# Attention and mixture-of-experts block on one core: the routing starts sixteen units later, the slot lists are built over 52 units, and the last batch's output loads follow them

## What is computed

```python
xn = _layernorm(x)
# attention, 16 heads of 32: causal, with an ALiBi bias
scores = einsum('bhqd,bhkd->bhqk', q, k) / sqrt(D) - slope * |i - j|
attn = softmax(scores) @ v  ->  @ Wo.T + bo
# experts: 8, of which each token takes 2
probs = softmax(xn @ gate_w.T); topw, sel = top_k(probs, 2); topw /= sum(topw)
gate_up = xn @ w1[e].T; act = silu(g) * u; expert_out = act @ w2[e].T
ffn = sum over the two experts of topw * expert_out
out = x + attn + ffn
```

## The kernel before, in words

| step | unit |
|---|---|
| routing parts 0 to 11 | 369 to 387 |
| `rank` and part 12; parts 13, 14, 15, 16 | 393; 395, 397, 399, 401 |
| `places` and `slots` of chunks 0 to 7 | 403, 411, 417, 423, 427, 431, 435, 439 |
| `lists` of chunks 0 to 7 | 409, 415, 421, 425, 429, 433, 437, 441 |
| `listr` | 443 |
| six `oload` and `xbo` of the last batch | 474 |
| windows 0 and 1 | 482 and 496 |

## Time and profile before

### The profile page before, as it was taken

How to read it: one execution, slowest core, us unless ns; L and a number is a source line. 1 busy time by engine, 2 the same in 40 slices (tenths; PEclk the granted TensorE clock), 3 DMA queues, 4 the chain that set the end, 5 groups by cost and what they waited for, 6 DMA issues and landing times.

```text
span 1607.2 us, 35535 instructions
## 1 busy us (share of the span) xinstructions
PE 1469.5 (91%) x12763; PEld 892.2 (56%) x12763; DVE 1042.5 (65%) x2500; ACT 888.6 (55%) x2020; POOL 568.5 (35%) x595
## 2 busy tenths in 40 slices
PE   4899989998898999999899898999789999999995
PEld 2565545654565555556555466555356656656662
DVE  7887786666878767777788877777243333333331
ACT  5677686665768767676776465777122222222221
POOL 5111232121123213113222233221217777777675
PEclk9999999998999999999999899999899999999998
DMA  7355231442433255443214233145777889788893
GB/s 258 103 140 133 86 107 50 121 123 79 131 93 110 66 146 149 124 131 92 80 59 123 84 97 91 39 146 140 274 189 123 134 126 146 131 138 132 127 143 46
DMA packets 171350, 193.28 MB, mean 120 GB/s; under 512 B 87536, under 2 KB 121072, under 8 KB 171056
## 3 DMA queue, kind: packets, MB, share of 16 engines
q1 hardware_dynamic: 143760, 151.67, 34.6%
q0 software_dynamic: 26128, 37.24, 14.2%
q10 hardware_dynamic: 1296, 2.11, 0.3%
HBM read 93.45 MB, written 53.74 MB: 92 GB/s over the span
## 4 chain that ended last, share of the span: by engine, by line
PE 66%; DVE 11%; issue 6%; DMA 5%; SPq 4%; ACT 3%; POOL 2%; POOLq 0%; DVEq 0%; ACTq 0%
PE S L1224 15%; PE T L1147 11%; PE O L1163 7%; PE S L1104 5%; PE S L1136 5%; PE M L1104 4%; PE M L1255 4%; PE O L1255 4%; DVE arena L1528 4%; SPq L979 4%; PE M L1186 2%; DMA out<-arena 2%; PE S L1121 2%; DVE arena L1544 2%; PE S L1186 1%
## 5 line engine op out<-in xcount | busy, mean ns | idle before, releaser
L1528 DVE CUSTOM_DVE_ANT_0 arena<-S,cF,nsl 128x1024 f32<-128x1024 f32 (+7 forms) x512 | 413.1, 811 | 70.3 <-PE S L1136 48.5
L1725 ACT ACTIVATE arena<-arena,mneg 128x1024 f32<-128x1024 f32 (+7 forms) x512 | 395.6, 773 | 57.2 <-DVE mneg L1528 56.6
L1147 PE MATMUL T<-cF,arena 128*128 128x128 f32 x2304 | 366.3, 280 | 66.1 <-ACT arena L1742 37.3
L1742 ACT ACTIVATE arena<-T 128x512 f32<-128x512 f32 (+3 forms) x532 | 241.6, 467 | 250.7 <-PE T L1147 247.9
L1147 PEld LDWEIGHTS T<-cF,arena 128*128 128x128 f32 x2304 | 267.7, 142 | 169.3 <-issue 49.0
L1224 PE MATMUL S<-arena 128*128 x1704 | 269.8, 315 | 10.0 <-issue 9.9
L1881 POOL DMA_INDIRECT out<-arena x142 | 222.1, 1564 | 107.6 <-ACT arena L1788 57.9
L1224 PEld LDWEIGHTS S<-arena 128*128 128x128 f16 x1704 | 167.7, 98 | 109.1 <-issue 11.3
L1544 DVE COPY arena<-T 128x512 f32<-128x512 f32 (+3 forms) x300 | 153.2, 514 | 108.3 <-PE T L1147 106.5
L1163 PE MATMUL O<-arena 128*32 128x128 f32 (+1 forms) x3328 | 213.6, 333 | 6.8 <-DVE arena L1564 5.7
L1136 PE MATMUL S<-arena 96*128 96x512 f16 (+3 forms) x768 | 212.8, 331 | 3.1 <-DVE mneg L1528 1.8
(11 more groups left out here) (190 smaller groups left out, 1821.6 us busy)
## 6 DMA issues: line engine op xcount, KB each, us to landing
arena<-arena SPq DMA_DIRECT2D x192, 128.0 KB, 2.4
arena<-in_w1T SPq DMA_DIRECT2D x64, 352.0 KB, 3.5
arena<-in_x SPq DMA_DIRECT2D x64, 256.0 KB, 3.5
w_d<-arena SPq DMA_DIRECT2D x32, 352.0 KB, 2.9
arena<-w_d SPq DMA_DIRECT2D x16, 704.0 KB, 6.7
arena<-in_w2T SPq DMA_DIRECT2D x32, 256.0 KB, 2.9
out<-arena SPq DMA_DIRECT2D x32, 256.0 KB, 3.0
xn_d<-arena SPq DMA_DIRECT2D x24, 256.0 KB, 2.2
```

Of the source, the lines that this page charges most:

```text
L1147: tp = pe.transpose(z[:, (c - c0) * P:(c - c0 + 1) * P], ring[u % 4][:, c * P:(c + 1) * P], idf)
L1528: dve.tensor_tensor_reduce(ring[r][:, 0:w], SBK[o.bank["score", u]][:, 0:w], rel[:, S - w:S], nsl[:, hh:hh + 1], 3.0e38, ALU.add, ALU.min, ...
L1725: act.activation(ring[r][:, 0:w], ring[r][:, 0:w], ACT.Exp, bias=mneg[:, m:m + 1], scale=-1.0, accum_out=rs[:, k, c:c + 1]).then_inc(sems[ ...
L1742: act.activation(PT[k][:, h, to_:to_ + gap * (c1 - c0 - 1) + 1:gap, :], TB[o.bank["tr", u, i]][:, 0:n].rearrange("p (c n) -> p c n", n=P), ...
```

## The change

`routing()` is cut in two at the point where the lists begin. The first half (parts 0 to 16) begins at u = 385 instead of 369, with the same stride of two. The second half becomes a generator of its own, `lists()`, which begins at u = 428 with a stride of three. `o_steps` of the last batch begins at unit 495 instead of 474 (384 + 96 + 15 instead of 384 + 96 - 6). No instruction is added or taken away.

```diff
@@ -418,6 +418,8 @@
         yield
         add("route", 16)
         yield
+
+    def lists():
         for c in range(NT // 4):
             add("places", c)
             add("slots", c)
@@ -608,14 +610,15 @@
-        jobs.append((u0 + 96 + (9 if b + 1 < B else -6), 1, 1, u0 + 128 + 44, o_steps(b)))
+        jobs.append((u0 + 96 + (9 if b + 1 < B else 15), 1, 1, u0 + 128 + 44, o_steps(b)))
...
     split_jobs = [w_max(), w_scales(), w_split()]
-    jobs.append((32 * 11 + 17, 2, 1, 32 * 15, routing()))
+    jobs.append((32 * 12 + 1, 2, 1, 32 * 13 + 12, routing()))
+    jobs.append((32 * 13 + 12, 3, 1, 32 * 15 + 14, lists()))
     jobs.append((32 * 15 + 2, 1, 1, 32 * 15 + 4, win(0)))
```

## The result

| | before | after |
|---|---|---|
| median (11 runs each) | 1607.26 us (1600.77 to 1614.79) | 1612.44 us (1607.31 to 1619.51) |
| ratio | | 1.0034, 95% interval 1.0019 to 1.0050 |
| span of the profiled execution | 1607.2 us | 1610.7 us |

The change makes the kernel slower by 0.34%, 3 to 8 us. The profiled executions differ by 3.5 us only: that of the kernel before lies 1.7 us above its median, and single executions of one kernel lie up to 14 us apart. Of the 3.5 us, units 368 to 479 hold 2.5 and what follows unit 480 0.9.

The account below looks back on a forecast made before the run. TensorE and VectorE share the bound in the attention, VectorE through the routing. Terms -2.0 + 1.2 - 3.9 - 5.9 + 15.3 + 0.9 sum to +5.6 us, 1612.8 us against the median 1607.26; range 1603 to 1619.

Parts of the forecast that it names:

- Points 1 to 3: Units 368 to 383 lose the routing, -2.0 us; 384 to 411 get it, with 1.5 us wait for `rank`, +1.2.
- Points 4 and 5: Units 412 to 427 without lists, -3.9 us; units 428 to 443 with only chunks 0 and 1, -5.9 us.
- ruler: Last batch's units beside the same units one batch earlier, without routing or lists; priced lists at 2.1 us a chunk.
- Point 6: Units 444 to 479 get chunks 2 to 7: 2.1 us each for 2 to 4, +6.3; 3.0 each after, +9.0.
- D: Slower by clock: TensorE partly at 1.2 GHz again at `rank` or late lists, 2 us; outside the sum.
- Point 7: `listr` in unit 482, where VectorE is nearly full, costs +0.9 us.
- Point 8: Six late output loads and GpSimd's additions cost nothing; additions end near 1102, 4 us before the next `aT`.
- C: Slower by the tail: late output loads make `aT` of unit 487 wait behind `xbo`; +5 us on top, 1618 us, chance 0.07.
- the contention that the Trainium skill states: VectorE instructions with two SBUF inputs exclude GpSimd's SBUF reads; tables-to-`lists` wait over 4 us, 4.5 a chunk, sum +10.
- rival A: Faster: three units between tables and products remove 8.4 us of TensorE waits; late chunks cost 1.5 us; 1602 us, chance 0.23.
- Rival B: No change: the bounding engines' work is the same wherever it stands; 1607 us, give or take 3, chance 0.25.
- The other signs: Units 464 to 479 not under 28 us, 384 to 411 within 76 to 82; `rank` wait 1.5; late-chunk TensorE idle 1 to 2.

Follow-up runs that it names:

- lists late alone: The changed kernel with the routing back at unit 369, lists and output loads staying late: 1609.84 us, ratio 1.0015.
- tables only: The changed kernel with chunks 5 to 7 reduced to VectorE's two tables, no products or sums; executed once, units 464 to 479 take 26.7 us.
- gap of four: The kernel before with each list chunk's products at least four units behind its tables, tables at units 403 to 443: 1609.55 us, ratio 1.0017.
- routing late alone: The kernel before with the routing from unit 385 and the lists right behind at their old spacing, output loads unmoved: 1615.78 us, ratio 1.0062.
- gap late: As the kernel with four units between tables and products, but three units and lists beginning 13 units later, tables at 416 to 446: 1614.39 us, ratio 1.0040.
- rank apart: The changed kernel with `rank` and routing part 12 six units behind part 11, parts 13 to 16 six later; executed once, units 368 to 479 262.0 us.

## Why the prediction was right or wrong

It forecast 1612.8 us, and 1612.44 was measured, slower as forecast. The agreement to 0.4 us is luck: the profiled span grew by 3.5 us, not 5.6, and terms of the sum were off in both directions. At unit 480 the forecast stood at +4.7 us and the trace at +2.6. The measured 5.2 come of these 2.6, of 0.9 behind that unit, and of the 1.7 us by which the profiled execution of the kernel before lay above its median while that of the changed kernel is its median. By its own dates:

| unit begins | predicted | measured |
|---|---|---|
| 384 | 851.4 | 851.5 |
| 412 | 930.9 | 930.9 |
| 428 | 966.6 | 962.3 |
| 444 | 1003.9 | 997.3 |
| 464 | 1051.8 | 1047.6 |
| 480 | 1082.9 | 1080.8 |

- **Points 1 to 3, the routing (+1.2 - 2.0 us): right in size.** 34.8 and 79.4 us were measured for 34.7 and 79.5. The routing costs the same early and late (146.0 and 145.7 us with nothing else). The meeting at rank, sized 1.5 us with bounds 0 and 3, is worth 2.0 by the run that takes it apart. That the routing's new place was no worse than the old although it had this meeting was not in the argument; units 412 to 427 took less for it.
- **Points 4 and 5, units 412 to 443: too slow by 6.6 us.** This is the step that failed. I took the same units one batch earlier as the bare time, 35.7 and 33.1 us. The bare ones are 31.5 to 34.3 and, by 32.9 - 2.0, 30.9. So the price of a list chunk in the kernel before came out too low as well: 2.1 us by the ruler, 2.6 by the runs that leave chunks out (2.4 at the full clock). Of the 6.6 us, 3.6 are the ruler's (68.8 against 34.3 + 30.9), and 2.9 are that units 412 to 427 begin with TensorE ahead behind the late routing (31.4 against 34.3). The ruler's premise, the same weight splitting in both batches, does not hold: one batch earlier the split tiles are 704 wide, not 512, and ScalarE waits longer for their stores (9.1 us against 3.1). Its copies of turned scores stand behind that in its queue, and TensorE waits for them 6.0 us instead of 1.6. These 4.4 us are of the size of the ruler's 3.6; no run takes them away by themselves. First the ruler, 641.2 to 710.0 us, then units 412 to 443 in the run with the lists late alone, which hold two chunks:

```profile
L1605 DVE SCALAR_TENSOR_TENSOR arena<-arena,sc x8: 945/949/952, 647.1 to 705.8; 128x704 f16<-128x704 f32 x8
...
ACT arena L1761 <- DMA w_d<-arena: 9.1, 3, 4.3
...
PE T L1147 <- ACT arena L1742: 6.0, 7, 2.5
```

```profile
L1608 DVE SCALAR_TENSOR_TENSOR arena<-arena,sc x8: 744/746/1712, 931.0 to 990.5; 128x512 f16<-128x512 f32 x5, 96x512 f16<-96x512 f32 x3
...
ACT arena L1764 <- DMA w_d<-arena: 3.1, 1, 3.1
...
PE T L1150 <- ACT arena L1745: 1.6, 3, 0.7
```

- **Point 6, units 444 to 479: too fast by 4.5 us.** Chunks 2 to 4 cost 2.8 us each (50.4 - 42.0), not 2.1, which follows from the same error. Chunks 5 to 7 cost 3.7, not 3.0. The bounds, 1.5 and 4.5, held it. Of the 2.1 us that three chunks lay beyond the middle, 1.6 are the clock, as D had it: the products of chunk 6 lasted 3.59 us instead of 2.18. At the full clock a chunk is 3.2 us: 1.8 for the products, 1.0 for the tables, 0.4 for the wait.
- **Point 7, `listr` at 0.9 us: not there.** Units 480 to 495 take 22.7 or 22.8 us with it or without, and 24.0 in the one trace (tables only) that has a stretch at 1.2 GHz there.
- **Point 8, output loads at nothing: right.** The run that moves them alone shows no difference, the additions run from 1094.5 to 1102.0 us, and the fear in C did not come true.
- **On the contention that the Trainium skill states** (SBUF — State Buffer, Who interferes with whom), I had said that it speaks for 4.5 us a chunk. The trace of before agrees with the rule in kind: of GpSimd's two products of chunk 4 the first, beside VectorE's tables, took 2.05 us, and the second, which began behind them (the prediction has both beside them), 1.14. Together they took 3.27 us in the pure units as elsewhere, but TensorE's wait for them was one of 1.1 us; what made the chunk dear was VectorE and TensorE.
- **TensorE's idle time ahead of the lists** was misread. The 8.4 us that the view of line 1206 gives, and that I used as TensorE's wait in rival A, adds up the waits of the weight loads and of the matmuls of the same blocks: 4.8 and 3.6 us in the waits of the kernel before. TensorE stood idle for 3.6 us. Rival A fails twice over: there was less to gain, and the run with a gap of four shows that taking the wait away gains nothing by itself.

```profile
PEld M L1206 <- issue: 4.8, 4, 2.4
...
PE M L1206 <- issue: 3.6, 3, 2.2
```

- **Rival B, no change,** has a true premise: in units 368 to 479 TensorE is busy for 241.6 us before and 241.0 after. It fails because the idle time is not the same wherever the work stands: 19.9 and 23.1 us.
- **The other signs.** Units 464 to 479 took over 28 us and units 384 to 411 lay between 76 and 82, as asked. VectorE waited 1.22 us for `rank`, for the 1.5 forecast. TensorE's idle time ahead of the lists was nothing for chunks 1 to 4, but for 5 to 7 it was 1.1 us once and not 1 to 2 us each.

What stays open is why the routing late alone, with two units between tables and products, is dearer by 5.6 us than the run with the gap late, which has nearly the same density (32 and 33 units). One more stretch at the lower clock is worth about 1.5 of it. For the rest the idle time ahead of the products (8.8 us against none) is of the right size, but the gap of four against the kernel before, where 3.6 us of idle time made no difference, speaks against taking the one for the other. No run here separates them.

## What to carry to other kernels

Side work put between the steps of a loop in which two engines run in lockstep costs more the less room the loop's own step has: here 2.0 us a chunk where it was spread over 52 units ahead of the pure attention, 3.2 where both engines were full (3.7 with a fall of the clock), and there the two engines' shares came one after the other instead of hiding each other. Spread such work widely, but end it before the stretch without room begins; moving it from a busy place into the busiest one is a loss even if the waits around it go away. And measure the bare loop by leaving the work out: the same stretch one batch earlier was 1 to 4 us off in 35, since it held other side work. Before a stretch is compared with another, look whether the clock fell in one of them.

## What the runs showed of the hardware

- A stretch of attention repeats from trace to trace to 0.1 or 0.2 us (units 464 to 479 without lists: 22.0 to 22.2 in nine traces), unless TensorE's granted clock fell to 1.2 GHz in one of them. A fall of 3.4 us costs 1.5 us in units 444 to 463 (51.9 against 50.4) and 1.6 in units 464 to 479 with lists (33.1 against 31.5).
- Whole executions of the same kernel spread over 16 us (1597.06 to 1613.04 in 23 runs of the kernel before, at a mean granted clock of 0.984 and 0.975). In the traces most of the spread lies in the first 256 units (522.8 to 532.4 us), where the stretches at 1.2 GHz fall differently from run to run: the run with the gap of four has one of 6.8 us at 51.2 us, that with the gap late none before 363.8.
- In the changed kernel TensorE stood still for 1.66 us ahead of 1062.34, and the products of chunk 6, 2 us later, took 3.59 instead of 2.18 us, in part at 1.2 instead of 2.4 GHz. With the lists alone late the same block took 3.61 us. In the run with rank apart, the same steps with the same wait of 1.66 us came without the fall, and the block took 2.21. So the wait alone does not bring it about; what does is not shown.
